# Softmax steps over two images on partition halves, with small array tiles, in a fused vision-transformer layer

## The reference, cut to what matters

```python
h = tokens(x)                                   # 16 x 36 x 192
q, k, v = split(h @ w_qkv.T)                    # 12 heads x 64
q = q * rsqrt(norm(q, axis=heads) + eps); k = k * rsqrt(norm(k, axis=heads) + eps)
scores = softmax(q @ k.T / scale[head])         # per image: 36 x 36, 12 heads
h = layernorm(h + (scores @ v) @ w_out.T + b_out)
h = layernorm(h + moe(h))                       # top 2 of 8, weights softmax of the two logits
```

## Time and profile before

| | |
|---|---|
| median of 3 runs | 155.0 us (152.06, 155.44, 155.0) |
| span of the profiled execution, first to last instruction | 149.9 us |
| TensorE / VectorE / ScalarE / GpSimd busy | 140.9 / 105.6 / 95.4 / 87.3 us |
| granted TensorE clock, mean | 0.997 |

### The profile page before, as it was taken

One profiled execution on the slowest core, in us unless ns is written; L12 is line 12 of the kernel. 1 busy time (PEld: TensorE's weight loads), 2 busy tenths in 40 slices (PEclk: granted clock), 3 DMA queues, 4 the chain that ended last, 5 costly groups with the idle time before them and its releaser, 6 DMA issues. The chain is left out here.

```text
span 149.9 us, 3224 instructions
## 1 busy us (share of the span) xinstructions
PE 140.9 (94%) x1155; PEld 127.3 (85%) x1156; DVE 105.6 (70%) x248; ACT 95.4 (64%) x215; POOL 87.3 (58%) x99
## 2 busy tenths in 40 slices
PE   6999899999999899999979999999999999999960
PEld 2789899999966678797958898999999998999950
DVE  0047699269278879999876537779768797678852
ACT  3064989985497996667788988225555545344631
POOL 7703079670449596999997657638625434333602
PEclk9999999999999999999999999999999999999998
DMA  5899855600203001203400000000000000000021
GB/s 134 329 411 403 332 132 187 210 0 0 74 35 107 2 4 23 84 4 105 109 0 0 0 4 2 0 2 4 0 0 0 0 4 0 0 2 4 0 66 52
DMA packets 4399, 10.60 MB, mean 71 GB/s; under 512 B 480, under 2 KB 1312, under 8 KB 4384
## 3 DMA queue, kind: packets, MB, share of 16 engines
q1 hardware_dynamic: 4384, 10.41, 20.7%
HBM read 9.96 MB, written 0.44 MB: 69 GB/s over the span
## 5 line engine op out<-in xcount | busy, mean ns | idle before, releaser
L463 POOL TENSOR_TENSOR reg_r<-reg_p,reg_r 128x324 fp32r<-128x324 f32 (+1 forms) x23 | 19.1, 832 | 20.6 <-ACT reg_r L722 20.6
L383 POOL TENSOR_TENSOR reg_w<-stage,reg_w 128x768 fp32r<-128x768 f32 x12 | 22.5, 1885 | 14.1 <-ACT reg_w L529 5.4
L722 ACT ACTIVATE reg_r<-reg_p 128x324 fp32r<-128x324 f32 (+1 forms) x24 | 10.6, 443 | 23.8 <-DVE reg_p L1077 23.8
L1054 DVE TENSOR_SCALAR reg_q<-ps,bup 128x324 f32<-128x324 f32 (+1 forms) x24 | 12.3, 513 | 5.3 <-PE ps L1291 5.1
L1077 DVE SCALAR_TENSOR_TENSOR reg_p<-reg_q 128x324 f32<-128x324 f32 (+1 forms) x24 | 13.8, 575 | 2.2
L1287 PE MATMUL ps<-reg_r,reg_w 128*128 128x324 f32 (+1 forms) x48 | 14.9, 311 | 0.0
L1290 PE MATMUL ps<-reg_r,reg_w 128*128 128x324 f32 (+1 forms) x48 | 14.2, 295 | 0.0
L1288 PE MATMUL ps<-reg_r,reg_w 128*128 128x324 f32 (+1 forms) x48 | 14.2, 295 | 0.0
L1291 PE MATMUL ps<-reg_r,reg_w 128*128 128x324 f32 (+1 forms) x48 | 14.2, 295 | 0.0
L1289 PE MATMUL ps<-reg_r,reg_w 128*128 128x324 f32 (+1 forms) x48 | 14.2, 295 | 0.0
L713 ACT ACTIVATE reg_q<-ps,sm 128x324 f32<-128x324 f32 (+1 forms) x24 | 11.7, 486 | 0.5 <-PE ps L1291 0.5
(11 more groups left out here) (217 smaller groups left out, 452.5 us busy)
## 6 DMA issues: line engine op xcount, KB each, us to landing
reg_x<-xw_in SPq DMA_DIRECT2D x5, 416.0 KB, 5.7
stage<-w_gu_a SPq DMA_DIRECT2D x4, 384.0 KB, 3.1
stage<-w_gu_b SPq DMA_DIRECT2D x4, 384.0 KB, 3.0
stage<-w_qkv_a SPq DMA_DIRECT2D x3, 384.0 KB, 7.6
stage<-w_qkv_b SPq DMA_DIRECT2D x3, 384.0 KB, 8.1
stage<-w_down SPq DMA_DIRECT2D x3, 384.0 KB, 3.1
wout<-w_out SPq DMA_DIRECT2D x1, 576.0 KB, 9.9
reg_x<-xw_in SPq DMA_DIRECT2D x1, 272.0 KB, 2.7
```

The lines of the kernel that those rows point to most:

```text
L383: nc.gpsimd.tensor_tensor(dst[:, 1, :], raw, f(dst[:, 0, :]), ALU.subtract).then_inc(s_wlop, 1)
L463: nc.gpsimd.tensor_tensor(acts[:, n % NACT, 1, 0:w], act_f[:, n % 4, 0:w], f(acts[:, n % NACT, 0, 0:w]), ALU.subtract).then_inc(s_alo, 1)
L1054: nc.vector.tensor_scalar(upw[:, n % 4, 0:w], ps[:, e_bank(n) + 1, 0:w], bup1[:, c:c + 1], LIMIT + 1, ALU.add, ALU.min).then_inc(s_u, 1)
```

## The change

The masks go. A step now takes two images and all twelve heads, eight steps in all (`NU` = 8). Image 0 of a step has its 36 queries on partitions 0 to 35, image 1 on 64 to 99 (`LANES` = 100). A score matmul is 64 rows by 36 (or 64) columns by 36 moved columns and sits in one 64-by-64 quarter of the array; there are 24 of them in a step, and 24 in the weighted sum. The transposes take two heads at once (`pairs` is a permutation), so that the transposed probabilities of two heads lie on two partition halves. For that the values are wanted on both halves as well: SyncE copies rows of `V` to `v2` by 36 DMAs. ScalarE takes exp in one pass over both banks, and TensorE subtracts the maximum in both. V has five tiles of 126 tokens (the last 72) where it had six. The first norms are for 144 tokens.

In turn `k` TensorE has `subtract_max(k)`, `p_transpose(k-2)`, in turns 4 and 5 `project(k-4)`, `scores(k+1)`, `weighted(k-2)`. VectorE has `sum_recip(k)` ahead of `row_max(k+1)`. The layer norm's transposes, the router work and the whole `gate_up`s follow the last steps.

```diff
-GRP = IMG * SEQ
-NU = 2 * NG - 1
+NU = B // 2
+ST = 2 * SEQ
+FST = 2 * ST
+LANES = 64 + SEQ
+VSIZES = [126, 126, 126, 126, 72]
...
+            for k in range(len(pieces)):
+                for u in {12: (0, 1, 2, 3, 4), 13: (5, 6, 7)}.get(k, ()):
+                    values(u)     # wait s_vev; 2 DMAs for each piece of v_pieces(u)
...
 def scores(u):
+                for i in range(3):
+                    for r in range(2):
+                        for b, img in ((0, 0), (1, 1), (0, 1), (1, 0)):
+                            m = head_of(b, i, r) // 2
+                            rows, c, t = slice(64 * b, 64 * b + 64), SEQ * (2 * i + r), o + SEQ * img
+                            n = (64, SEQ)[img]
+                            last = mm(ps[64 * img:64 * img + n, bank + b, c:c + SEQ], qk[rows, m, t:t + n],
+                                      qk[rows, NP + m, t:t + SEQ], start=(i == 0 and r == 0), stop=False,
+                                      skip_group_check=True)
 def subtract_max(u):
+                for b in range(2):
+                    last = mm(ps[0:LANES, bank + b, 0:6 * SEQ].rearrange("p (h j) -> p h j", h=6), ident_r[0:LANES, 0:LANES],
+                              mx_r[0:LANES, u % 2, 6 * b:6 * b + 6].unsqueeze(2).to_broadcast([LANES, 6, SEQ]),
+                              start=False, stop=True, skip_group_check=True)
 def p_transpose(u):
+                for j in range(NP):
+                    last = mm(ps[0:LANES, PT_BANK, ST * j:ST * j + LANES],
+                              probabilities(u)[0:LANES, 128 * j:128 * j + LANES], pairs[0:LANES, :], start=True, stop=True,
+                              is_transpose=True)
 def weighted(u):
+                pe.wait_ge(s_v2[u], 32 * len(v_pieces(u)))
+                for i in range(3):
+                    for a in range(2):
+                        for r, b in ((0, 0), (1, 1), (0, 1), (1, 0)):
+                            rows, j, c = slice(64 * r, 64 * r + SEQ), 3 * b + i, SEQ * a
+                            last = mm(ps[64 * b:64 * b + 64, O_BANK + r, ST * i + c:ST * i + c + SEQ],
+                                      v2(2 * u + a)[rows, 64 * j:64 * j + 64], PT[rows, u % 2, ST * j + c:ST * j + c + SEQ],
+                                      start=True, stop=True)
...
 VectorE
+            for k in range(0, NU):
+                sum_recip(k)
+                if k + 1 < NU:
+                    row_max(k + 1)
+                if k in (4, 5):
+                    ln1_stats(k - 4)
+                if k + 2 < NU:
+                    q_norm(k + 2)
+                if k in (4, 5):
+                    ln1(k - 4)
+            h1_lo(0)
+            h1_lo(1)
+            ln1_stats(2)
+            ln1(2)
+            read_logits(0)
+            rank(0)
+            router_weights(0)
+            read_logits(1)
+            rank(1)
+            h1_lo(2)
+            router_weights(1)
             read_logits(2)
             rank(2)
...
 ScalarE, after the loop
+            pt_evac(6)
+            o_evac(6)
+            pt_evac(7)
+            h1_evac(2)
+            w_hi(12)
+            o_evac(7)
+            choose(0)
+            nc.scalar.preload_act_table_set("gelu_apprx_sigmoid_and_others")
+            choose(1)
             expert(0)
             choose(2)
...
 GpSimd
             for k in range(0, NU):
+                probs(k)
+                if k + 3 < NU:
+                    k_norm(k + 3)
+                if k in (4, 5):
+                    root(k - 4, TSIZES[k - 4], s_ve, s_rstd)
+                if k in (2, 3, 4, 5):
+                    w_lo(k + 6)
...
 TensorE
             for k in range(0, NU):
                 subtract_max(k)
+                if k >= 2:
+                    p_transpose(k - 2)
+                if k in (4, 5):
+                    project(k - 4)
                 if k + 1 < NU:
                     scores(k + 1)
+                if k == 7:
+                    h1_transpose(0)
+                    h1_transpose(1)
+                    project(2)
+                if k >= 2:
+                    weighted(k - 2)
+            p_transpose(6)
+            logits(0)
+            logits(1)
+            weighted(6)
+            p_transpose(7)
+            h1_transpose(2)
+            project(3)
+            weighted(7)
+            gate_up(0)
             logits(2)
+            gate_up(1)
             gate_up(2)
             h1_transpose(3)
```

More of the change, by code:

```diff
@@ L195, in vit_layer @@
         s_piece = [sem(f"s_piece{i}") for i in range(17)]
+        s_v2 = [sem(f"s_v2_{u}") for u in range(NU)]
         (s_small, s_wo, s_out, s_rows, s_onehot, s_rawa, s_lgb, s_smlo, s_xb, s_w1hi, s_w1lo) = [
@@ L250, in w_count @@
             return k - 1 + sum(1 for i in P_WD if i <= k)
-        uses = [("qk", m) for m in range(10)] + [("sum", 0), ("qk", 10), ("qk", 11), ("v", 0), ("v", 1), ("v", 2), ("sum", 1)]
-        uses += [("v", g) for g in range(3, NG)]
+        uses = [("qk", m) for m in range(10)] + [("sum", 0), ("qk", 10), ("qk", 11), ("v", 0), ("v", 1), ("sum", 1), ("v", 2)]
+        uses += [("v", g) for g in range(3, NV)]
         slot = {use: 2 * (n % 4) for n, use in enumerate(uses)}
@@ L785, in _ @@
             expert(1)
-            o_evac(10)
+            w_hi(13)
             expert(2)
+            w_hi(14)
             h1_evac(3)
@@ L1373, in _ @@
             v_proj(1)
+            norm_sum(1)
             v_proj(2)
-            norm_sum(1)
             v_proj(3)
             def scores(u):
-                g, j = divmod(u, 2)
-                n, o = SIZES[g], OFFS[g]
-                b = s_bank(u)
+                o, bank = ST * u, s_bank(u)
+                if u == 0:
+                    pe.wait_ge(s_vev, 3)
+                    pe.wait_ge(s_kn0, 1)
+                elif u == 1:
+                    pe.wait_ge(s_vev, 4)
+                else:
+                    pe.wait_ge(s_e, u - 1)
+                pe.wait_ge(s_qn, u + 1)
+                if u:
+                    pe.wait_ge(s_kn, u)
+                for i in range(3):
+                    for r in range(2):
+                        for b, img in ((0, 0), (1, 1), (0, 1), (1, 0)):
[5 more added lines that the diff above has]
+                                      skip_group_check=True)
+                last.then_inc(s_s, 1)
@@ L1718 @@
     wqkvT = arr(L0_attn_w_qkv).T.reshape(D, 3, PD).transpose(1, 0, 2)
-    w_outT = arr(L0_attn_w_out).T.reshape(NC, 128, D).transpose(1, 0, 2)
+    rows = [64 * head_of(b, i, r) + n for r in range(2) for b in range(2) for i in range(3) for n in range(64)]
+    wqkvT = np.stack([wqkvT[0], wqkvT[1], wqkvT[2][:, rows]])
+    rows = [64 * head_of(b, i, r) + n for r in range(2) for i in range(3) for b in range(2) for n in range(64)]
+    w_outT = arr(L0_attn_w_out).T[rows].reshape(NC, 128, D).transpose(1, 0, 2)
     def tiles(a):
```

432 lines of the change are left out of this document (129 added, 303 removed).

## The result

| | before | after |
|---|---|---|
| median | 153.9 us (4 runs, 152.06 to 155.44) | 159.5 us (4 runs, 158.93 to 160.32) |
| ratio | | 1.046, 95% interval 1.038 to 1.055 |
| span of the profiled execution | 149.9 us | 157.7 us (time 159.49) |
| granted TensorE clock, mean | 0.997 | 0.925 |

The profiled run of the changed kernel lies 1.8 us above its span, so the 149.9 us of before belong to a run of some 151.7 us, near the quickest of the four and not near the median. The kernel before runs at two levels, which go with its clock (of 17 runs beside the last experiment, twelve with a mean granted clock of 0.995 or more took 151.2 to 152.3 us, five with 0.967 to 0.971 took 155.0 to 155.4), and every ratio here compares only the quicker runs of either kernel, for before in this table 152.06 and 152.78, so it is not the ratio of the medians.

The account below looks back on a forecast made before the run. TensorE was taken to bound the kernel, its matmul groups adding up. Lateness of 0.8 us plus 1.0 for stretching made 1.8 us on the 149.9 span, so 151.7; with 5.1 carried over, 156.8 us, range 152.5 to 162.

Parts of the forecast that it names:

- The PE work of the steps: TensorE's matmul groups in the steps: eight turns of 2.95 us, 23.6 in all, 3.3 us less than before.
- The loop through the other engines: Subtract, exp, sum, reciprocal, maximum in a row: a turn takes at least 2.5 us, which sets turns 0 and 1.
- the sixth V projection: Two halves of 0.87 us dropped from steps 0 and 1, where TensorE waits for the maximum anyway: worth nothing.
- GpSimd ... 3.9 us in turns 2 and 3 ... Costed at nothing: GpSimd's probabilities, K norm and weight piece exceed those turns, but slack absorbs it; without slack, 0.9 us for each of two turns.
- q_norm's stretch: VectorE's q_norm, slowed beside GpSimd's multiplying ahead of the next sum, lengthens the loop: 1.0 us added, bounds 0 and 3.
- The price of the tiles: Scores and weighted sum in 64-by-64 tiles: 2.05 us a turn, midway between 1.4 (four at a time) and 2.7 (two).
- rivals 2 and 3: Tiles four at a time, 3.9 us less, 152.9 (chance 0.22), or two at a time, 4.5 more, 161.3 (chance 0.22).
- rival 3: Tiles work two at a time: a turn has 3.6 us, 4.5 us more in all, 161.3, slower; chance 0.22.
- rival 4: A floor of 25 ns per score or sum record: pair 2.4 us, turn 3.3, 2.3 us more, 159.1; chance 0.10.
- The timeline: Steps added up: subtraction 0 at 44.0, loop twice to 49.0, 0.5 us wait for project(1), weighted(7) through at 79.85.
- The tail: Router work after the last step leaves TensorE idle 3.6 us ahead of gate_up(0), 0.7 ahead of gate_up(1); h1_transpose(3) 0.8 late.
- The V copies: SyncE's 36 copies of V rows, 0.33 us per issue, 12 us in all between 36 and 51: cost nothing.

Follow-up runs that it names:

- before_v5_early: Kernel before with both halves of the sixth V projection moved ahead of the loop, so TensorE idles in steps 0 and 1; 158.3 us, ratio 1.032.
- fill01: Changed kernel with half a V projection done once more in each of turns 0 and 1, into an unread bank; 159.6 us, ratio 1.046.
- fill_wlo: Changed kernel with repeated half V projections filling turns 0 and 1, and GpSimd's w_lo(8) to (11) moved to turns 4 to 7; 155.1 us, ratio 1.021.
- fill_wlo_tail: fill_wlo plus, at the tail, h1_lo(2) ahead of rank(1) on VectorE and choose(0) ahead of o_evac(7) and w_hi(12) on ScalarE; 153.7 us, ratio 1.009.
- tail_fill: Changed kernel with eight float32 matmuls into an unread bank between weighted(7) and gate_up(0), the stall itself staying; 158.6 us, ratio 1.042.
- quarter_major: fill_wlo_tail with scores and weighted-sum matmuls ordered six in a row per array quarter instead of going round the quarters; 183.6 us, ratio 1.200.
- best2: The last experiment: fill_wlo_tail with more operations reordered on all four compute engines, then four waits this made mended; 151.4 us, ratio 0.986.

## Why the prediction was wrong, point by point

It said 156.8 and most likely no change; it was slower, with 159.5.

*The step that failed* stands in "The PE work of the steps" and "The loop through the other engines": the sixth V projection "filled time in which PE waits for DVE's maximum anyway: worth nothing", and turns 0 and 1 "go by this loop". I saw PE idle for 1.1 of 2.5 us in two turns, and for 3.6 us at the tail, and priced the idle time alone. Every later duration I took from rows at a granted clock of 1.00, though nothing in a sum with such gaps says that it stays there. before_v5_early shows the fall without the rest of the change, and fill01 with fill_wlo that it comes with the idle time and that the tiles run at the full clock without it. The price: weighted(7) started at 84.39 with the clock lost and at 79.87 with it held (fill_wlo_tail), 4.5 us for both edits of the steps; at the tail 1.2 us (tail_fill). Together that is 5.7 us, where my span was 6.0 us short.

*Hidden by it* was "GpSimd ... 3.9 us in turns 2 and 3 ... Costed at nothing". GpSimd's own lateness cost nothing; its hold on VectorE did. q_norm's stretch, which I gave 1.0 us (bounds 0 and 3), was up to 2.9 us for one operation (fill01). Covered by a PE at half speed it cost little, but it was the second thing to drop the clock.

*The price of the tiles*: "midway, 2.05" was 1.64 us, with 1.4 for four at a time. The range of rivals 2 and 3 held it; rival 3, two at a time, falls with that number and with quarter_major's factor of 2.3; rival 4's 25 ns a record falls too, since 96 records in 1.64 us are 17 ns each. (Its sum was also off: five turns 0.35 us longer are 1.75 us and not 2.3.) The scores alone, 0.65 to 0.69 us up to the weighted sum for 24 matmuls, come to 27 to 29 ns for a float32 matmul of two records. The Trainium skill's floor of some 25 ns between starts ("TensorE: Matmul & The Clock Gate", Wait — 56ns, not 53.3ns?) fits if it counts matmuls and not records; I had applied it to records. The Trainium skill's statement that tiles work independently ("TensorEngine Tiling (Array Packing)", Key Properties) agrees with the 2.3 of quarter_major, if neighbours in the queue lie in different tiles.

*The timeline*: near the mark where the clock held. Subtractions 0 and 2 at 44.0 and 49.0 (44.03, 49.18), and weighted(7) to end at 79.85, against 80.7 in fill_wlo_tail. Part of that is luck: the pair was priced 0.4 us too high in each of the turns that go by it, and the waits were priced too low, project(1)'s at 0.5 for 1.52, those ahead of scores(4) and of subtraction 7 at nothing for 0.81 and 0.76.

*The tail*: right in mechanism and size. 3.6 us ahead of gate_up(0) were 3.2, with rank(1) behind choose(0) behind o_evac(7); 0.7 ahead of gate_up(1) were 0.46. Against my times gate_up(0) was 5.1 us late and h1_transpose(3) 6.1. From one to the other it took 8.9 us where I had 7.8; with the clock held (tail_fill, 88.36 to 95.76) it took 7.4, so the lateness between them is the clock's. down(0), which I had as just covered, waited 0.40 us for GpSimd.

*The V copies*: nobody waits for one in the trace. Each of the 36 issues took 0.71 us in the median and not 0.33, so SyncE was busy with them up to 67 us, and pieces 13 to 16 came that late. Costed at nothing, and nothing by the trace of the changed kernel. Fewer or larger copies were not tried.

*The frame*: I carried 5.1 us from span to time where 1.8 was right. That took 3.3 us off the error by chance; my span of 151.7 was 6.0 us short of 157.7.

What stays open is which idle time costs the clock. Ahead of project(1), 1.52 us passed without a fall in the changed kernel and in fill_wlo_tail, while a fall followed 1.09 us in fill_wlo; and four runs of one kernel differ (fill_wlo_tail: mean clock 0.966 to 0.998). So it stays open, too, how much of best2's spread an order could still remove.

## What to carry to other kernels

Before you write "hidden, costs nothing" beside work that a change takes out of an engine's idle time, ask what TensorE does in its place: if it idles, cost the rows behind it at either clock level and give the lower one a chance of its own. When an edit that should gain moves nothing, look at the trace before dropping the theory, since a second cause of the same kind may stand right behind the first, and only both edits together show it. And a step that gets shorter is worth only as much as the chain that used to run beside it allows.

## What the runs showed of the hardware

- Two idle times of TensorE of 0.94 us, 2.2 us apart, were followed by 1.2 GHz for ten microseconds (before_v5_early); in the profile of the kernel before, where a projection filled them, the same work ran at 2.4 GHz. Not each such wait does it: one of 1.52 us passed at the full clock in two traces.
- The order of small matmuls alone is worth a factor of 2.3: 48 records of scores to the next group in 0.83 us round the four quarters, in 1.89 us quarter by quarter.
- A VectorE product of two SBUF operands takes 0.60 us alone and 3.54 us beside two GpSimd products in a row; it ended 0.5 us after the second. The reductions from PSUM beside GpSimd kept their 0.61 us.
